# Attention over a 48x48 image: GpSimd in place of VectorE divides each block's output by its sums

## The reference

```python
xn = (xg - mean) * jax.lax.rsqrt(var + EPS)          # 32 groups of 16 channels
xn = xn.reshape(b, c, T) * gn_w[None, :, None] + gn_b[None, :, None]
qkv = jnp.einsum('oc,bct->bot', qkv_w, xn) + qkv_b[None, :, None]
weight = jnp.einsum('bct,bcs->bts', q * scale, k * scale)
weight = jax.nn.softmax(weight.astype(jnp.float32), axis=-1)
a = jnp.einsum('bts,bcs->bct', weight, v).reshape(b, c, T)
hout = jnp.einsum('oc,bct->bot', proj_w, a) + proj_b[None, :, None]
return (xn + hout).reshape(b, c, h, w)
```

## Time and profile before

| | |
|---|---|
| runs | 3774.66, 3774.83, 3775.08 us, median 3774.83 |
| profiled execution | 3774.18 us, its span 3772.5 us |
| granted TensorE clock | 0.997 of full speed |
| busy, share of the span | PE 98%, POOL 80%, ACT 76%, DVE 60% |
| a block of the first three pairs | some 35.9 us |
| the chain that ended last, by engine | PE 91%, ACT 3%, DMA 2%, DVE 2% |

### The profile page before, as it was taken

One profiled execution on the slowest core, in us unless ns is written; L12 is line 12 of the kernel. 1 busy time (PEld: TensorE's weight loads), 2 busy tenths in 40 slices (PEclk: granted clock), 3 DMA queues, 4 the chain that ended last, 5 costly groups with the idle time before them and its releaser, 6 DMA issues.

```text
span 3772.5 us, 74528 instructions
## 1 busy us (share of the span) xinstructions
PE 3699.3 (98%) x30004; PEld 2263.6 (60%) x30004; DVE 2246.3 (60%) x2820; ACT 2867.9 (76%) x4037; POOL 3001.7 (80%) x1639
## 2 busy tenths in 40 slices
PE   6999999999999999999999999999999999999998
PEld 4565565655856556565675656556567565656556
DVE  4566557656555565765646565666655656565653
ACT  2777777787577777778757777777876777777885
POOL 0788888888388888888838888888874888888994
PEclk9999999999999999999999999999999999999999
DMA  2000012011400001201140000110223000000014
GB/s 80 14 23 22 21 36 69 23 56 38 146 21 19 24 23 32 73 19 58 44 139 19 23 23 17 52 53 27 68 63 104 23 21 21 22 19 19 20 37 138
DMA packets 133673, 165.02 MB, mean 44 GB/s; under 512 B 61648, under 2 KB 110800, under 8 KB 132816
## 3 DMA queue, kind: packets, MB, share of 16 engines
q1 hardware_dynamic: 133328, 160.26, 13.5%
HBM read 122.17 MB, written 38.04 MB: 42 GB/s over the span
## 4 chain that ended last, share of the span: by engine, by line
PE 91%; ACT 3%; DMA 2%; DVE 2%; issue 1%; SPq 1%; POOL 0%; POOLq 0%; ACTq 0%; DVEq 0%
PE oacc L611 29%; PE scores L590 23%; PE pool_bank L538 13%; PE aux_banks L560 12%; PE pool_bank L550 7%; PE scores L690 4%; PE pool_bank L577 1%; ACT probs L795 1%; ACT scores L808 1%; DVE maxima L911 1%; DMA out<-probs 1%; PE scores L538 1%; DMA neg_rows<-neg_cols 1%; POOL denom L1157 0%; DVE o_norm L1018 0%
## 5 line engine op out<-in xcount | busy, mean ns | idle before, releaser
L1157 POOL TENSOR_TENSOR denom<-denom,probs 128x768 f32<-128x768 f32 x1536 | 2825.5, 1840 | 425.0 <-ACT probs L795 235.0
L911 DVE TENSOR_REDUCE maxima<-aux_banks 128x2 f32<-128x512 f32 x1728 | 1656.0, 958 | 1314.9 <-PE aux_banks L560 1281.9
L795 ACT ACTIVATE probs<-scores 128x768 f32<-128x768 f32 x1728 | 1311.2, 812 | 676.1 <-PE scores L590 668.1
L808 ACT ACTIVATE scores<-seeds 128x768 f32<-128x768 f32 x1728 | 1342.6, 823 | 19.3 <-PE scores L598 10.0
L611 PE MATMUL oacc<-probs,vals 128*64 128x384 f32 x6912 | 1283.0, 492 | 0.0
L611 PEld LDWEIGHTS oacc<-probs,vals 128*64 128x64 f32 x6912 | 455.0, 136 | 523.3 <-issue 381.9
L560 PE MATMUL aux_banks<-k_hi,q_hi 64*128 64x512 f32 (+1 forms) x3456 | 684.0, 391 | 20.7 <-DVE maxima L911 18.8
L560 PEld LDWEIGHTS aux_banks<-k_hi,q_hi 64*128 64x128 f32 x3456 | 322.8, 183 | 548.9 <-issue 443.8
L590 PE MATMUL scores<-q_hi,k_hi 64*128 64x384 f32 x3456 | 599.6, 343 | 17.3 <-ACT scores L808 17.0
L590 PE MATMUL scores<-q_lo,k_hi 64*128 64x384 f32 x3456 | 587.6, 335 | 0.0
L590 PE MATMUL scores<-q_hi,k_lo 64*128 64x384 f32 x3456 | 587.5, 335 | 0.0
(11 more groups left out here) (91 smaller groups left out, 1476.4 us busy)
## 6 DMA issues: line engine op xcount, KB each, us to landing
seeds<-neg_rows SPq DMA_DIRECT2D x96, 384.0 KB, 3.5
xtile<-x SPq DMA_DIRECT2D x72, 384.0 KB, 3.2
att<-o_norm SPq DMA_DIRECT2D x96, 192.0 KB, 1.9
probs<-x SPq DMA_DIRECT2D x24, 768.0 KB, 4.5
out<-probs SPq DMA_DIRECT2D x24, 768.0 KB, 3.7
xtile<-att SPq DMA_DIRECT2D x12, 768.0 KB, 4.6
att_raw<-att SPq DMA_DIRECT2D x12, 768.0 KB, 6.3
neg_rows<-neg_cols SPq DMA_DIRECT2D x384, 0.8 KB
```

Of the source, the lines that this page charges most:

```text
L795: a(prob(s).rearrange("p (h n) -> p h n", n=N), scores[:, s % 2, :, 0:N], ACT.Exp, scale=SCALE).then_inc(probs_ready, 1)
L808: a(scores[:, s % 2, :, 0:N], seeds[blk % 2][:, :].rearrange("p (e n) -> p e n", n=N), ACT.Copy).then_inc(seeded, 1)
L911: v.tensor_reduce(maxima[:, :, qt, kc], aux_banks[:, :, 0:UNIT_KEYS[kc % 2]], AX.X, ALU.max)\
L1157: gp.tensor_tensor(acc, acc, prob(s), ALU.add).then_inc(added, 1)
```

## The change

VectorE keeps the first three pieces of `take_recip`. The multiplication becomes `normalize_block` on GpSimd, with the same three waits. GpSimd does it behind its addition of step 11 of the next block, and for the last block of a batch behind all additions. SyncE's put moves to the same step, 11 in place of 10. In SyncE's loop over the steps `send_max` stands ahead of the put, and it too belongs to step 11. The semaphore `o_normed` is now raised by GpSimd.

```diff
-    PIECES = 4
+    PIECES = 3
@@ fin_steps
-            return [t, t + 1, t + 2, t + 4]
+            return [t, t + 1, t + 2]
@@ put_at
-            return {p * STEPS + fin_steps(j)[-1]: p * CH + j for p in range(PAIRS) for j in range(CH)
+
+            return {p * STEPS + fin_steps(j)[-1] + 3: p * CH + j for p in range(PAIRS) for j in range(CH)
                     if (p, j) != (PAIRS - 1, CH - 1)}
@@ take_recip
-                elif piece == 2:
+                else:
                     dve.wait_ge(cols_ready, PRIMED + n + 1)
                     dve.wait_ge(o_normed, PRIMED + n)
                     v.transpose(recip[:, :].rearrange("p (c r) -> p c r", r=32),
                                 recip_cols[:, :].rearrange("p (c o) -> p c o", o=1)
                                 .broadcast_to([128, N // 32, 32])).then_inc(recip_ready, 1)
-                else:
-                    dve.wait_ge(recip_ready, PRIMED + n + 1)
-                    dve.wait_ge(o_saved, PRIMED + n + 1)
-                    dve.wait_ge(att_out, PRIMED + 16 * n)
-                    v.tensor_tensor(o_norm[:, :], o_raw[:, :], recip[:, :], ALU.mult).then_inc(o_normed, 1)
@@ vector, start
-            for s in (o_normed, out_ready, cols_ready, recip_ready):
+            for s in (out_ready, cols_ready, recip_ready):
@@ gpsimd
-            pool.sem_inc(added, PRIMED)
+            def normalize_block(n):
+                pool.wait_ge(recip_ready, PRIMED + n + 1)
+                pool.wait_ge(o_saved, PRIMED + n + 1)
+                pool.wait_ge(att_out, PRIMED + 16 * n)
+                gp.tensor_tensor(o_norm[:, :], o_raw[:, :], recip[:, :], ALU.mult).then_inc(o_normed, 1)
+
+            for s in (added, o_normed):
+                pool.sem_inc(s, PRIMED)
@@ gpsimd, batch
                 for s in range(BSTEPS):
                     add(s, b)
+                    if s in PUT_AT:
+                        normalize_block(BLOCKS * b + PUT_AT[s])
+                normalize_block(BLOCKS * b + BLOCKS - 1)
```

## The result

The changed kernel takes 3768.97 us (median of 20 runs, 3767.17 to 3770.12); the kernel before, in 20 runs beside it, 3775.64 us. The ratio is 0.9981, with a 95% interval of 0.9975 to 0.9988: 6.7 us faster. The profiled executions have spans of 3772.5 and 3766.6 us, 5.9 us apart.

What follows compares the result with a forecast made beforehand. TensorE was taken as the bound, with GpSimd's queue deciding the last pair of the last batch. Costs 3.5 + 0.4 less gains 7.7 made -3.8 us: 3771.0 us for the median, forecast 3769 to 3773, range 3767.0 to 3777.2.

Steps and rivals of the forecast that it cites:

- What bounds the kernel: Whole kernel: TensorE busy 98%; relieving VectorE pays only where TensorE waits, loading GpSimd costs only where GpSimd is late.
- The statistics slots: Third block of pair 2, first three batches: VectorE also holds the next batch's statistics; removing the multiply gains 2.7 us.
- The seeds: After block 20, first three batches: sends of maxima now precede the put, so ScalarE's seeds come earlier; gain 3.35 us.
- The small excesses: Eleven other blocks, same two slots at the multiply: 0.05 to 0.22 us too long; gain 1.6 us in all.
- GpSimd ahead of the last pair: First three batches: GpSimd idles 425 us ahead of its additions, so one multiply more per block costs nothing.
- GpSimd in the last pair: Last pair of last batch: GpSimd works almost without pause; six multiplies cost 3.5 us, bounds 2.5 to 8.7.
- The last block's multiply: Projection: GpSimd's multiply waits out VectorE's low part, put 2.1 us later; mostly hidden by full DMA engines, cost 0.4 us.
- The rival that was weighed as likeliest to be slower: Last pair and projection: multiply dear on GpSimd, 1.5 us or more each; at 1.83 us, 3777.1 us; chance 0.16.
- offloading doesn't help: Rival: VectorE and GpSimd still exclude each other, only SyncE's order pays; +0.6 us, 3775.4; chance 0.12.
- the end is free: Rival: last pair and projection cost the low bound or less; -5.2 us, 3769.6, down to 3766; chance 0.17.
- The median: Whole kernel: 3771.0 us forecast for the median of the runs, from 3774.83 before.

Runs made afterwards that it cites:

- e5: Changed kernel, with every multiply that falls ahead of the last batch's last pair done twice on GpSimd; 3768.94 us.
- e6: Changed kernel, with GpSimd multiplying only in pair 2 and VectorE elsewhere, the put still behind the sends; 3767.63 us, ratio 0.9979.
- e1: Kernel before, with only SyncE's put moved to step 11, behind the sends of the maxima; VectorE keeps the multiply; 3772.45 us, ratio 0.9990.
- e7: Changed kernel, with GpSimd multiplying one column of 384, the rest of the block's output left at zero; 3764.84 us.
- e4: Changed kernel, with GpSimd doing each of the six multiplies in the last batch's last pair twice; 3775.38 us.
- e2: Changed kernel, with GpSimd multiplying one step earlier and the put back at step 10, ahead of the sends; 3790.2 us, ratio 1.0037.
- e11: Changed kernel, last pair's multiplies on VectorE; in five blocks there GpSimd skips the last of 17 additions, TensorE sums it instead; 3759.68 us, ratio 0.9956.

## Why the prediction was right, and where its terms were off

**What bounds the kernel.** Right. 168 us less on VectorE and 87 us more on GpSimd (e5) are both without effect where nobody waits.

**The statistics slots.** Forecast 2.7, traces 2.6, and e6, which moves only the multiplies of pair 2, has the same 2.6.

**The seeds.** Forecast 3.35, traces 3.7 in the changed kernel and 3.5 in e1, 2.6 to 3.2 in e1's medians. That in the last batch the same stall would bring nothing is shown by e1's unbroken run of 197.0 us, to within 0.4. The loads behind the put were to come some 7 us later and came 3.6 later (886.67 for 883.06); nothing hung on it.

**What was missed: 1.1 us in the coefficients' slots.** The sum looked for excess only in the two slots at the multiply. In block 4 of pair 2 of the kernel before slots 7 and 8 were too long as well (in the first batch 4.01 and 4.58 us, in the changed kernel 3.71 and 4.35). VectorE has small operations of four columns there, three with two SBUF inputs and one with a single one. The same one before and after:

```profile
704.33 1.68 DVE L978 TENSOR_TENSOR small<-small 128x4 f32<-128x4 f32 x1
```

```profile
703.67 0.23 DVE L979 TENSOR_TENSOR small<-small 128x4 f32<-128x4 f32 x1
```

Four columns took 1.68 us because the operation was ready just after one of GpSimd's additions had begun (704.17), and 0.23 where it came near the multiply's end. The operation with one SBUF input waited in the same way, and ended with an addition too; in the changed kernel it took 0.53 us. Before:

```profile
712.28 1.60 DVE L982 TENSOR_SCALAR small<-small 128x4 f32<-128x4 f32 x1
```

Counted from the block's first exponential, the operation is ready at 27.8 us in both kernels, and the addition beside it begins at 27.62 before and, behind the multiply, at 27.96 after. In e5 the additions are later by a further us; three of these four operations take 1.24, 1.49 and 1.07 us again, and still the two slots keep to their length, as VectorE had room for that much. In e7, where the multiply is nearly gone from both engines, they take 1.2 to 1.6 us, and the three blocks gain only 0.43 + 0.16 + 0.14 = 0.7 us. So some of the 1.1 us comes from where GpSimd's additions happen to fall, and not from VectorE's relief. What the prediction had wrong here is where it looked: it left the coefficients' slots out of its sum. **The small excesses** were read nearly rightly: 1.6 forecast, 2.3 in the traces, of which 0.5 us stands in the last blocks of the first three batches, where I had looked for none. No run isolates that part.

**GpSimd ahead of the last pair.** Nothing, as forecast; e5 adds a whole us more a block and it is still nothing. The prediction gave as the reason that a block's sum is read late. It did not count ScalarE's waits for additions there, 48.1 us in place of 7.2; they cost nothing, but a busier ScalarE would have had to pay for them.

**GpSimd in the last pair.** Forecast 3.5, measured 200.9 - 197.45 = 3.5. That the two agree to 0.1 us is luck in part. The multiply takes 1.007 us, not 0.97, so the term is 6 x 0.79 = 4.7 and not 4.5. The 99 additions of the run get back 1.4 us (184.2 us in all before, 182.8 after), not 0.9. And the pause within the run did not go: 0.43 us where 0.25 was, +0.2 in place of -0.1. 4.7 - 1.4 + 0.2 = 3.5. That the length of the multiply sets the cost is shown from both sides: e7 takes 0.82 us out of each and gets 4.9, e4 puts one more in and pays 6.4.

**The last block's multiply.** The collision came as described, 2.44 us for a forecast of 2.7 (1.75 + 0.97): the low part had a lead of 0.15 us. The cost was put at 0.4 and is -0.1 by the traces, within what profiled executions differ at the end (49.1 to 51.5 us in twelve kernels with the same additions there).

**The rival that was weighed as likeliest to be slower** (a multiply from 1.5 us up) falls with 1.007 us; by the prediction's own terms its case at 1.83 us is +2.2, not the +2.3 written. That offloading doesn't help falls with e6, which gains 5.4 us more than e1 does, each against its own kernel before. That the end is free is half true: the last pair isn't, the projection is.

**The median.** 3771.0 forecast, 3768.97 measured. The gain itself was under-forecast by more than these 2.0 us: 3.8 forecast, 6.7 measured, since the kernel before ran at 3775.64 beside the changed one and not at 3774.83. Of the 2.9 us the two traces have 2.1, as their spans are 5.9 us apart: 1.55 ahead of the last pair and 0.5 at the end. The other 0.8 is within what single profiled executions differ from the medians.

## What to carry to other kernels

An engine's total is not what a change is worth: 168 us taken from VectorE were worth about 6 us ahead of the last pair (9.75 less e1's 3.86), a quarter of the multiplies (pair 2) brought most of that, and 3.5 us went again in the last pair. GpSimd is about twice as slow at this multiply as an undisturbed VectorE (1.007 against 0.55 us), and still the move pays, since neither length was on the path in most blocks. When a step moves to another engine, ask what its transfer stands ahead of in the issuing queue: here it is worth about 3.5 us to issue one put behind the sends and not ahead of them (e1), and with a late producer in front it is worth 21 us (e2). And look for the stretch in which the receiving engine never waits, since there every operation costs its length less only what it hides (0.96 us for 1.00 in e4); that stretch is also where the next gain lies (e11).

## What the runs showed of the hardware

- On GpSimd a multiply of 128x384 took 1.007 us and one of 128x1 0.19 us, beside 1.83 for an addition of 128x768. From the three an estimate is 0.19 us and 2.1 ns for each further column.
- Two independent operations of GpSimd follow each other in 0.96 us where one takes 1.00 (e4); an addition that waits for the one before starts 0.14 us after its end.
- A VectorE operation of four columns with two SBUF inputs took 1.68 us beside an addition of GpSimd's and 0.23 us at another phase; and GpSimd's multiply took 2.44 us behind a VectorE operation of 1.72 us that had started 0.15 us earlier. Both ways the one that comes second waits until the first ends, or nearly so.
- A VectorE operation of four columns with one SBUF input (a multiply and an addition of constants) waited for the end of one of GpSimd's additions as well: 1.60 us before, 1.49 in e5, 0.53 in the changed kernel. A second SBUF input is not needed for such a wait.
- A store of 768 KB took 8.2 to 9.1 us to land when it was issued 13.1 us after the last addition, while two loads were under way, and 5.6 to 6.8 us when issued 14.8 to 15.4 us after it. Its landing time in the end differed by less than 1.7 us.
